# State scan of a fused vision kernel: groups of states and decays moved from odd to even columns

## The reference, cut to what matters

```python
dA = delta[..., None] * A
A_bar = jnp.exp(dA)
B_bar = (A_bar - A) / dA * delta[..., None] * Bproj[:, :, None, :]
def step(h, inp):
    a, b, c, xl = inp
    h = a * h + b * xl[..., None]
    y = jnp.einsum('bn,bdn->bd', c, h)
    return (h, y)
```

## Time and profile before

| | |
|---|---|
| median of 3 runs | 8852.1 us (8850.1 to 8852.6) |
| span of the profiled execution | 8851.0 us (1.1 us under the median of the runs; the profile has no other time of its own) |
| last stage, first scan to last | 3421 to 8745 us of the span |
| busy over the whole span | PE 86%, DVE 69%, POOL 67%, ACT 49% |
| busy in one unit of the middle, 192 us | POOL 174.9, DVE 167.8, PE 161.8, ACT 93.8 us |

### The profile page before, as it was taken

One profiled execution on the slowest core, in us unless ns is written; L12 is line 12 of the kernel. 1 busy time (PEld: TensorE's weight loads), 2 busy tenths in 40 slices (PEclk: granted clock), 3 DMA queues, 4 the chain that ended last, 5 costly groups with the idle time before them and its releaser, 6 DMA issues.

```text
span 8851.0 us, 86861 instructions
## 1 busy us (share of the span) xinstructions
PE 7640.3 (86%) x31228; PEld 3191.2 (36%) x31228; DVE 6123.7 (69%) x6499; ACT 4307.9 (49%) x7642; POOL 5969.8 (67%) x2484
## 2 busy tenths in 40 slices
PE   8999999869999966688888788888888888878887
PEld 5444444224444422233333333333333333333333
DVE  2555555531333335988888888888888888888884
ACT  3666666643444423444445544444544444544442
POOL 0111111137666605999989999998999998999995
PEclk9999999989999977789999889999889999889888
DMA  1111111135444412233223233223333333323321
GB/s 37 39 41 44 40 44 33 38 68 107 95 99 99 99 41 91 92 117 112 102 96 124 94 123 118 102 94 116 104 108 114 112 102 101 120 96 125 114 100 51
DMA packets 356855, 786.60 MB, mean 89 GB/s; under 512 B 70437, under 2 KB 282806, under 8 KB 348936
## 3 DMA queue, kind: packets, MB, share of 16 engines
q1 hardware_dynamic: 320376, 690.75, 25.5%
q0 software_dynamic: 21712, 51.75, 2.3%
q10 hardware_dynamic: 14336, 38.54, 1.3%
HBM read 597.36 MB, written 183.35 MB: 88 GB/s over the span
## 4 chain that ended last, share of the span: by engine, by line
PE 35%; DVE 14%; ACT 6%; issue 5%; POOL 3%; DMA 0%; SPq 0%; DVEq 0%; ACTq 0%; POOLq 0%
PE ps L1627 7%; PE ps L1735 6%; DVE v L1980 6%; PE ps L1634 6%; DVE v L1971 5%; PE ps L1632 5%; PE ps L1673 3%; ACT ps L1862 3%; PE ps L1623 2%; PE ps L1738 2%; PE ps L1736 2%; POOL v L1582 1%; POOL v L1594 1%; PE ps L1677 1%; DVE dl L1961 1%
## 5 line engine op out<-in xcount | busy, mean ns | idle before, releaser
L1980 DVE TENSOR_TENSOR_SCAN v<-ps,v 128x898 f32<-128x898 f32 x1344 | 2725.2, 2028 | 92.4
L1594 POOL TENSOR_TENSOR v<-v,ct 128x1792 f32<-128x1792 f32 x672 | 2474.3, 3682 | 441.6 <-ACT st L1823 441.6
L1582 POOL TENSOR_TENSOR v<-xr,bt 128x1792 f32<-128x1792 f32 x672 | 2473.0, 3680 | 98.6 <-DMA xr<-h_by_channel 98.6
L1862 ACT ACTIVATE ps<-dr,aa 128x448 f32<-128x448 f32 x2688 | 1585.8, 627 | 1537.0 <-DVE v L1980 1519.7
L1971 DVE SCALAR_TENSOR_TENSOR v<-ps,aa,v 128x448 f32<-128x448 f32 x2688 | 1690.1, 671 | 548.2 <-ACT ps L1862 520.7
L237 POOL DMA_DIRECT2D tokens<-ob x448 | 235.4, 532 | 1660.1 <-ACT ob L457 1611.9
L1735 PE MATMUL ps<-w_or_w,gm 128*112 128x384 f32 x1792 | 721.0, 551 | 371.2 <-DVE gm L2057 278.7
L1673 PE MATMUL ps<-v,dg 128*32 128x448 f32 x5376 | 703.4, 598 | 204.1 <-POOL v L1594 109.6
L1735 PEld LDWEIGHTS ps<-w_or_w,gm 128*112 128x112 f32 x1792 | 334.6, 197 | 769.4 <-DVE gm L2057 320.4
L1627 PE MATMUL ps<-h,w_or_w 128*128 128x448 f32 x1344 | 537.2, 550 | 15.3 <-DVE gm L2024 15.3
L1632 PE MATMUL ps<-x,wpa 128*128 128x448 f32 x1008 | 445.2, 577 | 16.6 <-ACT h L1788 9.4
(11 more groups left out here) (325 smaller groups left out, 12021.6 us busy)
## 6 DMA issues: line engine op xcount, KB each, us to landing
xr<-h_by_channel SPq DMA_DIRECT2D x168, 896.0 KB, 7.3
dr<-delta_by_channel SPq DMA_DIRECT2D x168, 896.0 KB, 6.4
x<-tokens SPq DMA_DIRECT2D x252, 224.0 KB, 5.2
tokens<-ob POOLq DMA_DIRECT2D x448, 112.0 KB, 2.4
w_or_w<-in_w SPq DMA_DIRECT2D x29, 1536.0 KB, 6.4
w_or_w<-centred_w SPq DMA_DIRECT2D x27, 1536.0 KB, 6.5
h_by_channel<-h SPq DMA_DIRECT2D x112, 336.0 KB, 11.0
delta_by_channel<-dl SPq DMA_DIRECT2D x112, 336.0 KB, 4.7
```

Source lines behind the costliest of these rows:

```text
L1582: tt(v[:, n % RING, :, 1:T + 1], xr[:, dc % 2, 1:].rearrange("p (i t) -> p i t", i=4), bt[:, q:q + 1, :].to_broadcast([128, 4, T]), ALU.mu ...
L1594: tt(v[:, n % RING, :, 1:T + 1], v[:, n % RING, :, 1:T + 1], ct[:, q:q + 1, :].to_broadcast([128, 4, T]), ALU.mult).then_inc(s_cm, 1)
L1862: fn(decay(g), dr[:, dc % 2, g, :], ACT.Exp, scale=aa[:, 4 * k + g:4 * k + g + 1]).then_inc(s_a, 1)
L1980: nc.vector.tensor_tensor_scan(row, flat[:, 1024 * pair:1024 * pair + 2 * T + 2], row, 0.0, ALU.mult, ALU.add).then_inc(s_sc, 1)
```

## The change

In the last stage each group gets two columns ahead of its data in place of one. Groups of `v` become 450 columns long, with data from column 2, 452, 902 and 1352; the start state lies in the second of the two columns, and the first one is set to zero once by a new memset on POOL. Decays lie at columns 2 and 452 of each pair. `xr` loses its spare column, so that both buffers are read (and written by their DMA) from an even column, 0 and 1792. The scan starts at the start state of the first group, now column 1, and is 899 columns long in place of 898, over both the pair of decays and the pair of groups. Three waits on `s_set` ask for 7 in place of 6.

```diff
         def decay(g):
-            at = g // 2 * 1024 + g % 2 * (T + 1)
-            return flat[:, at + 1:at + T + 1]
+            at = g // 2 * 1024 + g % 2 * (T + 2)
+            return flat[:, at + 2:at + T + 2]
...
-        xr = sb("xr", [128, 2, 4 * T + 1])
+        xr = sb("xr", [128, 2, 4 * T])
...
-        v = sb("v3", [128, RING, 4, T + 1])
+        v = sb("v3", [128, RING, 4, T + 2])
...
-                sp.dma_start(xr[:, dc % 2, 1:],
+                sp.dma_start(xr[:, dc % 2, :],
...
-            sp.wait_ge(s_set, 6)
+            sp.wait_ge(s_set, 7)
...
-                tt(v[:, n % RING, :, 1:T + 1], xr[:, dc % 2, 1:].rearrange("p (i t) -> p i t", i=4), bt[:, q:q + 1, :].to_broadcast([128, 4, T]),
-                   ALU.mult).then_inc(s_v, 1)
+                tt(v[:, n % RING, :, 2:T + 2], xr[:, dc % 2, :].rearrange("p (i t) -> p i t", i=4),
+                   bt[:, q:q + 1, :].to_broadcast([128, 4, T]), ALU.mult).then_inc(s_v, 1)
...
-                tt(v[:, n % RING, :, 1:T + 1], v[:, n % RING, :, 1:T + 1], ct[:, q:q + 1, :].to_broadcast([128, 4, T]),
+                tt(v[:, n % RING, :, 2:T + 2], v[:, n % RING, :, 2:T + 2], ct[:, q:q + 1, :].to_broadcast([128, 4, T]),
...
+            pool.memset(v[:, :, :, 0], 0.0).then_inc(s_set, 1)
...
-                    last = mm(ps[32 * g:32 * g + 32, YB, 0:T], dg[:, 4 * k + g, :], v[:, n % RING, g, 1:T + 1],
+                    last = mm(ps[32 * g:32 * g + 32, YB, 0:T], dg[:, 4 * k + g, :], v[:, n % RING, g, 2:T + 2],
...
-                row = v[:, n % RING, g, 1:T + 1]
+                row = v[:, n % RING, g, 2:T + 2]
...
-                row = v[:, n % RING, 2 * pair:2 * pair + 2, :].rearrange("p g t -> p (g t)")
+                row = v[:, n % RING, 2 * pair:2 * pair + 2, :].rearrange("p g t -> p (g t)")[:, 1:]
...
-                nc.vector.tensor_tensor_scan(row, flat[:, 1024 * pair:1024 * pair + 2 * T + 2], row, 0.0, ALU.mult,
+                nc.vector.tensor_tensor_scan(row, flat[:, 1024 * pair + 1:1024 * pair + 2 * T + 4], row, 0.0, ALU.mult,
```

More of the change, by code:

```diff
@@ L1290, in decay @@
         def decay(g):
-            at = g // 2 * 1024 + g % 2 * (T + 1)
-            return flat[:, at + 1:at + T + 1]
+            at = g // 2 * 1024 + g % 2 * (T + 2)
+            return flat[:, at + 2:at + T + 2]
         def decays(pair):
-            row = flat[:, 1024 * pair:1024 * pair + 2 * T + 2]
-            return row.rearrange("p (g t) -> p g t", g=2)[:, :, 1:T + 1]
+            row = flat[:, 1024 * pair:1024 * pair + 2 * T + 4]
+            return row.rearrange("p (g t) -> p g t", g=2)[:, :, 2:T + 2]
         ident = sb("ident3", [128, 128])
@@ L1822, in keep_states @@
                 act.wait_ge(s_sc, 2 * others(n))
-                fn(st[:, 4 * k:4 * k + 4], v[:, n % RING, :, T], ACT.Copy).then_inc(s_st, 1)
+                fn(st[:, 4 * k:4 * k + 4], v[:, n % RING, :, T + 1], ACT.Copy).then_inc(s_st, 1)
             def start_states(i, k):
@@ L1832, in start_states @@
                     act.wait_ge(s_st, others(n - STEPS))
-                fn(v[:, n % RING, :, 0], st[:, 4 * k:4 * k + 4], ACT.Copy,
+                fn(v[:, n % RING, :, 1], st[:, 4 * k:4 * k + 4], ACT.Copy,
                    scale=0.0 if i % J3 == 0 else 1.0).then_inc(s_s0, 1)
@@ L1905, in _ @@
             act.wait_ge(s_pd, 16)
-            act.wait_ge(s_set, 6)
+            act.wait_ge(s_set, 7)
             act.preload_act_table_set(BOTH)
@@ L1990, in own_scan @@
                     dve.wait_ge(s_wt, 4 * n + g + 1)
[L1991 removed]
+                    nc.vector.tensor_tensor_scan(decay(g), decay(g), v[:, n % RING, g, 2:T + 2],
                                                  0.0 if first else st[:, 4 * k + g:4 * k + g + 1], ALU.mult,
@@ L1996, in own_scan @@
                 dve.wait_ge(s_sp, 4 * owned(n) + 2 * pair - 2)
-                tt(v[:, n % RING, 2 * pair:2 * pair + 2, 1:T + 1], decays(pair),
+                tt(v[:, n % RING, 2 * pair:2 * pair + 2, 2:T + 2], decays(pair),
                    ct[:, k % Q:k % Q + 1, :].to_broadcast([128, 2, T]), ALU.mult).then_inc(s_cv, 1)
@@ L2067, in _ @@
             nc.vector.memset(ps[:, 0:AR, :], 0.0).then_inc(s_set, 1)
-            dve.wait_ge(s_set, 6)
+            dve.wait_ge(s_set, 7)
             dve.wait_ge(s_pd, 5)
```

## The result

The changed kernel takes 8869.0 us (median of 14 runs, 8857.6 to 8874.9), the kernel before, in runs on the same chips, 8854.4 us (14 runs, 8843.0 to 8860.7). The ratio is 1.0018, with an interval of 1.0010 to 1.0026: slower by a little under 0.2%. I had forecast 0.1% faster, and a range that ended at 8855 us.

What follows compares the result with a forecast made beforehand. Middle units hang on a loop of PE, ACT and DVE; POOL matters in units 0, 1 and 27. -9.0 - 0.7 + 0.8 = -8.9 us on 8851.0 gives 8842.1; median 1.1 higher: 8843.2 us, range 8829 to 8855.

Steps and rivals of the forecast that it cites:

- What the odd column costs: POOL's products: an odd first operand costs 0.63 us on 1792 columns; from even columns each takes 3.36 us.
- Rival B: POOL's weigh_in: the 0.63 us belongs to xr's second buffer, not parity; POOL stays, 8853 to 8855 us; chance 0.12.
- The price on the path: Last stage: faster POOL products save 9.0 us at its start, including the first product's 0.6, and 0.7 in unit 27.
- DVE's share: Units 0 and 1: DVE's waits on POOL, 3.8 and 3.0 us, vanish before step (1, 4).
- The taps of chunk 1: Unit 1, PE: these matmuls wait for ACT's h of chunk 0 and start 9.0 us earlier, near 3618.8.
- The 0.7 us at the end: Unit 27: DVE's two waits on POOL go, saving 0.7 us.
- The faster weigh_out: POOL's weigh_out: with all groups even it drops from 3.68 to 3.36 us, 0.32 us a call.
- Rival A: Unit 1: PE's entry follows POOL alone, gaining 17.1 us, and ACT's decays 4.6 more; 8830.5 us; chance 0.2.
- Longer scans: DVE scans of 899 columns, 2.3 ns a column: +0.8 us on the path, +3.1 at the upper end.
- rival D: Middle units: PE's changed idle moments shift its clock, 0.3 us a unit, 8 us either way; it only widens the forecast.
- Rival C: DVE scans pay 0.31 us more for their odd start: +107 us, 8950 us; chance 0.05.
- The new memset, the transfers of x, the matmuls and ACT's decays: Last stage: memset hidden behind the wait for weights, transfers cost nothing, matmuls read as before, decays gain nothing counted.

Runs made afterwards that it cites:

- sweep: Not the kernel: POOL alone multiplies 128 x 1792 columns with the operands' and output's start columns varied; 3950 to 3959 ns or 3355 to 3360 ns.
- before_fast: The kernel before, with only x read from column 2 modulo 4 in both buffers, scans of 898 columns; ratio to before 0.9986, 8842.9 us.
- xr8: The changed kernel, with both buffers of xr read from column 2 modulo 4 in place of 0; ratio to before 0.9994.
- light_fast: The changed kernel, with x read from column 2 modulo 4 only in units 0, 1, 26 and 27; ratio to before 0.9998.
- mid_fast: The changed kernel, with x read from column 2 modulo 4 only in units 2 to 25; ratio to before 1.0018.
- xr8_v8: xr8 with groups 452 columns apart, all from column 2 modulo 4, 901-column scans, shared constants tile and larger memset; ratio to before 1.0006.
- after_xr1: The changed kernel with x's buffers as before (columns 1 and 1794); the rest of the change alone; ratio to before 1.0003.

## Why the prediction was wrong

**What the odd column costs** is the step that failed: "So an odd first operand costs 0.63 us on 1792 columns", and with it "After the change both read even columns only. I take 3.36 us for each". `weigh_in` measured 4.00 us and `weigh_out` 3.68. The two durations were right and the class was not. The trace showed two starts of x, 1 and 1794, which differ in parity, in their place modulo 4 and in their distance to B's rows, and weigh_out's 3.68 us fits all three. I wrote that all else was the same in these calls, which it was not, had no row that tells the three apart, and wrote down one; the sweep shows that it is the distance of the two inputs modulo 4 columns. Rival B named a near thing, that the 0.63 us might not belong to parity, but priced only the case in which nothing moves. That the fast half could become slow was missing among the rivals, and so the forecast had no term on the losing side for POOL (12 calls x 0.63 = 7.6 us in unit 0 alone). A change within 0.2% had a chance of 0.74, and the measured one is within it. That is luck: the sum that stood behind it had the wrong sign.

**The price on the path** came out near, by links that were only in part the ones I had named. The sum had 9.0 us at the start of the stage (0.6 of it from the first product), 0.7 at its end, and 0.8 to be paid for longer scans, all with both products fast. before_fast, with x fast in both buffers and the scans left alone, brings 8.5 us in units 0 and 1 and 8.8 in all from the first scan to the end (5420.7 against 5429.5 us); xr8 brings 167.5 + 191.8 - 164.0 - 187.2 = 8.1 us in units 0 and 1. Of the first product's 0.6 us, 0.26 reach the first scan: it starts 5.36 us after that product before, 5.11 us in before_fast. DVE's share held: the first scan of step (1, 4) comes 7.3 us earlier after the first scan of all, where I had 3.8 + 3.0 = 6.8. The taps of chunk 1 in before_fast show the link that did not hold (answer to the earlier trace rows; the first scan is at 3420.37):

```profile
3604.59 0.96 PE L1673 MATMUL ps<-v,dg 128*32 128x448 f32 x8 [0.66 <-POOL v L1594]
...
3616.07 2.52 PE L1623 MATMUL ps<-sq,jm 128*128 128x448 f32 x6
3618.43 2.56 PE L1632 MATMUL ps<-x,wpa 128*128 128x448 f32 x6
...
3617.07 0.62 ACT L1788 ACTIVATE h<-ps,pbias 128x448 f32<-128x448 f32 x1
```

PE comes to these taps in one unbroken run, and h of chunk 0 is written 0.7 us before they start. So they don't wait for h, as I had said; they wait for PE's own run, which begins with `weigh_out` of (1, 1). They start 198.1 us after the first scan, 206.3 before: 8.2 us gained where the sum had 9.0. The 0.7 us at the end did not come. light_fast has no wait of DVE on POOL there any more, and still it takes 281.4 us from the start of unit 27 to the end, as before does, behind a unit 26 of 190.5 us in both.

For the change as it is, unit 0 grew by what POOL lost: 12 fast calls made slow are 12 x 0.63 = 7.6 us, as POOL filled that unit already. light_fast and mid_fast show that POOL's work in units 2 to 25 is free, as I had said.

**The faster weigh_out** was to come from even groups. It did not come, and where it did (xr8_v8) it was worth nothing that shows. Rival A's 17 us needed PE to follow POOL alone. xr8_v8 refutes it: with both products at 3.36 us the taps of chunk 1 start 198.1 us after the first scan, just as in xr8 and before_fast, and units 0 and 1 together are 0.4 us longer than in xr8. There PE's run begins behind ACT's h of the last chunk of unit 0, which the chain leads back to DVE.

**Longer scans** were priced at 0.8 us on the path, 3.1 us at most. The instruction's share was right (2 ns each). The middle units hold more: by the 899-column kernels against the 898-column ones 0.13 to 0.37 us a unit, 3 to 9 us in 24 units. The size was off, and rival D, the shift of the loop (8 us either way), was the right name for it. It doesn't look like chance alone, as all six means at 899 columns lie above all three at 898; that it is the scans and not the stride of the groups is not shown.

**Rival C**, an odd start that slows the scan, is refuted: 2030 ns at the median from an odd column, 2028 from an even one. The rule of the Trainium skill about pairs that start on an odd word ("Vector Engine (DVE) Microarchitecture Reference", section "Measured stream behaviour on trn2") states 1.30 ns a column in place of 1.054 for them. Carried over to one long run, as the prediction did, it would have made the scan some 2250 ns, an estimate from that page; the 2030 ns of this trace don't agree with carrying it over.

**The new memset, the transfers of x, the matmuls and ACT's decays** cost nothing that shows, as predicted: the memset takes 0.14 us, and after_xr1 has all of them but the moved transfers, and unit 0 of before.

**Left open.** The middle units come mostly in lengths near 190.5, 191.8 to 192.0 and 193.0 us, and a kernel repeats a sequence of them. Windows over single units of the kernel before show the granted clock with them:

```profile
4354.84:4545.32 190.48, 160.18 (x571) 63.97 (x564) 167.62 (x174) 93.48 (x201) 174.73 (x49) 0.91 0.32 109
4545.32:4737.16 191.84, 161.10 (x554) 64.22 (x556) 167.64 (x174) 93.55 (x200) 174.78 (x49) 0.89 0.32 108
...
5119.46:5312.43 192.97, 162.63 (x554) 64.37 (x546) 167.64 (x174) 93.49 (x200) 174.71 (x49) 0.89 0.32 108
```

DVE, ACT and POOL do the same work in all three. The shortest has PE at 0.91 of its 2.4 GHz on average, the two longer ones at 0.89. But the mean clock doesn't settle the length: the very next unit has 0.91 in the earlier trace rows and takes 191.8 us. xr8_v8 has no unit near 190.5 us at all. That a few ns of scan shift the mixture through the moments at which the clock falls and rises is what I believe; no run here holds the clock still, so it is argued and not shown.

## What to carry to other kernels

When two calls of one form differ in time, write down all that differs between their operands, distances between operands too, before naming the cause; if the trace can't tell two readings apart, price the change under each of them, on the side where it loses as well. An engine that others wait for in two units of 28 is worth what it is worth in those two: take the gain from the waits on it there, unit by unit, and look for what comes just behind it (in xr8 POOL's two products still had 73% of the chain at the start, and making one of them faster took 0.4 us off unit 0). And before columns are added to an instruction of the loop, compare with leaving it alone: moving x alone by a few columns (before_fast) brought the best time.

## What the hardware showed that I had not expected

- POOL's product of two SBUF inputs, 128 x 1792 float32 with the second one's 448 columns read four times, takes 3.36 or 3.96 us alone (3.36 or 4.00 in the kernel), by the distance of the two inputs' start columns modulo 4: 0 or 1 is slow, 2 or 3 fast, 0.33 ns a column. The start of the output (0 to 3) changes nothing, nor does moving both inputs together.
- A scan of 899 columns on DVE costs the same from an odd as from an even column (2.03 us), with both inputs and the output odd.
- The middle units of this kernel, which wait on PE, ACT and DVE in turn, come in a few lengths. With scans of 901 columns in place of 898 DVE has 0.24 us more to do in a unit, and the mean unit is 0.66 us longer by another mixture of the same lengths; what else differs between these kernels is said above.
